# Gate and up products of the FFN by Strassen's scheme, with token pairs outside the weight chunks and the weights' low halves cut on GpSimd

## The reference

```python
def ffn(x, w_gate, w_up, w_down):          # x 2048 x 512, w_gate and w_up 512 x 2048, w_down 2048 x 512
    h = silu(x @ w_gate) * (x @ w_up)      # 2048 x 2048
    h = sparsify_2to4(h)                   # of each 4 neighbours in h the 2 largest magnitudes stay
    return layernorm(x + h @ w_down)
```

## Time and profile before

| | |
|---|---|
| time, median of 3 runs | 1092.13 us (1091.79 to 1092.42) |
| span of the profiled execution, first to last instruction | 1090.9 us |
| PE busy | 1037.0 us, 95% of the span |
| DVE busy | 738.5 us, 68% |
| ACT busy | 486.3 us, 45% |
| POOL busy | 294.7 us, 27% |
| mean granted TensorE clock | 0.992 of full speed |

### The profile page before, as it was taken

How to read it: one execution, slowest core, us unless ns; L and a number is a source line. 1 busy time by engine, 2 the same in 40 slices (tenths; PEclk the granted TensorE clock), 3 DMA queues, 4 the chain that set the end, 5 groups by cost and what they waited for, 6 DMA issues and landing times.

```text
span 1090.9 us, 18063 instructions
## 1 busy us (share of the span) xinstructions
PE 1037.0 (95%) x6022; PEld 839.6 (77%) x6023; DVE 738.5 (68%) x1769; ACT 486.3 (45%) x905; POOL 294.7 (27%) x496
## 2 busy tenths in 40 slices
PE   7889998999999885999999999999999999999996
PEld 6667776777777664888888888888888888888885
DVE  5898699778868986566747546545565536654666
ACT  5688488758857884222324222131222122221124
POOL 2186348545733641223210006000000000000224
PEclk9999999999999998999999999999999999999998
DMA  8877267727743732224541003210020000100102
GB/s 260 237 200 204 78 199 200 197 83 188 199 117 117 207 143 77 79 77 164 175 162 61 1 1 40 39 39 1 1 77 12 27 0 33 45 1 1 39 27 89
DMA packets 55216, 106.18 MB, mean 97 GB/s; under 512 B 6240, under 2 KB 8288, under 8 KB 55136
## 3 DMA queue, kind: packets, MB, share of 16 engines
q1 hardware_dynamic: 50256, 90.99, 29.7%
q0 software_dynamic: 4880, 14.18, 3.4%
HBM read 72.11 MB, written 30.94 MB: 94 GB/s over the span
## 4 chain that ended last, share of the span: by engine, by line
PE 57%; DVE 2%; ACT 1%; issue 0%; DMA 0%; POOL 0%; POOLq 0%; DVEq 0%
PE f_bank L53 55%; PE f_bank L1714 1%; PE f_bank L1722 1%; PE f_bank L1793 1%; PE f_bank L1738 0%; DVE ln_stats L1104 0%; DVE rows_kept L2150 0%; ACT rows_kept L1132 0%; DVE h L2116 0%; DMA rows<-sorted_dram 0%; DVE rows_kept L2139 0%; DVE h L2056 0%; DVE rows_kept L1111 0%; POOL out L1660 0%; ACT fsg L1936 0%
## 5 line engine op out<-in xcount | busy, mean ns | idle before, releaser
L1896 ACT ACTIVATE fsg<-f_bank 128x512 f32<-128x512 f32 x64 | 38.2, 598 | 295.6 <-PE f_bank L53 289.2
L2056 DVE TENSOR_TENSOR h<-f_bank,fsg 128x512 f32<-128x512 f32 x64 | 44.2, 691 | 181.6 <-PE f_bank L53 181.4
L714 ACT ACTIVATE probs<-bank,nmax 128x384 f32<-128x384 f32 (+3 forms) x256 | 131.7, 549 | 21.4 <-DVE nmax L899 19.3
L883 DVE CUSTOM_DVE_ANT_0 bank<-bank,mask 128x384 f32<-128x384 f32 (+3 forms) x256 | 122.9, 502 | 13.8 <-PE bank L510 13.0
L521 PE MATMUL bank<-ident,probs 128*128 128x128 f32 x640 | 108.7, 284 | 24.6 <-DVE pt_lo L908 10.7
L1137 POOL TENSOR_SCALAR ln_var<-ln_mv 128x1 f32<-128x1 f32 x39 | 8.9, 229 | 438.8 <-DVE ln_mv L1106 437.4
L908 DVE TENSOR_TENSOR pt_lo<-bank,pt_hi 128x512 f16<-128x512 f32 (+1 forms) x192 | 114.7, 598 | 16.7 <-ACT pt_hi L724 16.4
L724 ACT ACTIVATE pt_hi<-bank 128x512 f16<-128x512 f32 (+1 forms) x192 | 104.9, 546 | 23.5 <-PE bank L521 22.9
L53 PE MATMUL bank<-x_hi,w_qk 128*128 128x512 f32 x256 | 101.5, 414 | 6.7 <-DVE x_lo L913 6.3
L53 PE MATMUL f_bank<-wd_hi,hs_lo 128*128 128x512 f32 x256 | 100.0, 391 | 0.0
L53 PE MATMUL f_bank<-wd_lo,hs_hi 128*128 128x512 f32 x256 | 99.9, 390 | 0.0
(11 more groups left out here) (275 smaller groups left out, 2445.7 us busy)
## 6 DMA issues: line engine op xcount, KB each, us to landing
big_lo<-q_hi_dram SPq DMA_DIRECT2D x32, 256.0 KB
big_lo<-q_lo_dram SPq DMA_DIRECT2D x32, 256.0 KB
big_lo<-k_hi_dram SPq DMA_DIRECT2D x32, 256.0 KB, 3.8
big_lo<-k_lo_dram SPq DMA_DIRECT2D x32, 256.0 KB, 5.1
rows<-sorted_dram SPq DMA_DIRECT2D x19, 256.0 KB, 2.6
q_hi_dram<-q_hi SPq DMA_DIRECT2D x16, 256.0 KB, 3.0
q_lo_dram<-q_lo SPq DMA_DIRECT2D x16, 256.0 KB, 2.9
k_hi_dram<-k_hi SPq DMA_DIRECT2D x16, 256.0 KB, 3.5
```

What stands on the lines that cost most here:

```text
L714: ins = act.activation(probs[u % RP][:, at:at + cols(r)], S[u % SR][:, at:at + cols(r)], ACT.Exp, bias=nmax[:, r, c:c + 1])
L883: dve.tensor_tensor_reduce(out=S[u % SR][:, at:at + cols(r)], in0=S[u % SR][:, at:at + cols(r)], in1=mask[:, T - cols(r):T], scale=1.0, sc ...
L1896: act.activation(fsg[v % 2][:, :], GB[v % 2][:, :], ACT.Silu).then_inc(s_sg, 1)
L2056: dve.tensor_tensor(h[r % 2][:, j, :], UB[v % 2][:, :], fsg[v % 2][:, :], ALU.mult).then_inc(s_h, 1)
```

## The change

**Half-depth products.** For a pair of token blocks (r = 0, 1) and a pair of depth halves (each 256 of the 512 channels), the four products of gate and up against two token blocks are a 2x2 block product: weights (gate or up) by depth halves on one side, depth halves by token blocks on the other. Done plainly that is eight half-depth products; Strassen's scheme (in Winograd's form) makes it of seven, from sums and differences of weight blocks and of token blocks, and adds its results. A half-depth product here is 2 steps of depth by 3 matmuls, 6 matmuls. They are named 1 to 7, with a and b for two groups j; a round L holds 14 of them, 84 matmuls, where 96 stood for the same work. There are 16 rounds: 2 token pairs, by 4 chunks, by 2 halves of the groups.

**Order.** The token pair is now outermost, and each chunk's gate, up and down weights are loaded and cut twice, once for each pair. The tokens of the second pair are transposed, summed and cut between rounds 7 and 8. Down products come as 48 matmuls after the 14 products of a round: d = L - 2 after rounds 2 to 13, and the last four behind round 15. They use three PSUM banks in turn instead of four.

**ACT, for a round.** It copies six products out of PSUM (L2095), takes four SiLUs (L2100), makes magnitudes (L2112), copies the high half of what is kept (`kept_hi`, L2118, two of 1024 elements), and cuts 7 high halves of weights (`weight_hi`, L2046) for the next round and, in even rounds, 4 of down weights (`down_hi`, L2054).

**DVE, for a round.** Six additions of a product out of PSUM to a copy (`add_product`, L2288), two gated products with one input in PSUM (`gated_first`, L2295) and two with both in SBUF (`gated_second`, L2301), the comparisons, counts and choice of one block, the low half of what is kept (`kept_lo`, L2345, two of 1024), and four additions of the down product. It cuts no low halves of weights.

**GpSimd, for a round.** Four sums of weight blocks (L1729 to L1734) and seven low halves (`weight_lo`, L1739), and in even rounds four low halves of down weights (`down_lo`, L1747), each 128x512 with both inputs in SBUF. The raw weights have one buffer: the load of a round waits for the last low half of the round before.

**Buffers.** The high and low weights of a round have one place each, cut group by group (two products share a group) as PE is done with them.

The core of the diff, with the new functions:

```diff
-            def inner(c, v):
-                    matmul3(pe, banks[v % 2][:, :], lambda k, i: w[i][:, j, k, :], ..., KT).then_inc(s_done, 1)
+    ORDER = ("1a", "1b", "2a", "5a", "6a", "6b", "5b", "7a", "7b", "2b", "4a", "4b", "3a", "3b")
+    after_round = {L: [L - 2] for L in range(2, ROUNDS - 2)}
+    after_round[ROUNDS - 1] = [ROUNDS - 4, ROUNDS - 3, ROUNDS - 2, ROUNDS - 1]
+            def product(L, name):
+                for k in range(HALF):
+                    for a, b in ((0, 0), (0, 1), (1, 0)):
+                        ins = pe.matmul(to[:, :], aw[a][:, g, n, k * P:(k + 1) * P], x[b][:, k, :],
...
+            def down_product(d, ts=range(RW)):
+                    if t == 0:
+                        pe.wait_ge(s_hl, 2 * (d + 1))
+                        pe.wait_ge(s_dlo, J * (s + 1))
+            def weights_in(L):
+                if L > 0:
+                    sp.wait_ge(*wlo_ready(L - 1, GROUPS - 1))
...
+            def weight_sums(L):
+                pool.wait_ge(s_wraw, 64 * (L + 1))
+                pool.tensor_tensor(block_of(4), block_of(0), block_of(1), ALU.add).then_inc(s_wsum, 1)
+                pool.tensor_tensor(block_of(6), block_of(2), block_of(0), ALU.subtract).then_inc(s_wsum, 1)
...
+            def weight_lo(L, g):
+                i, j = group_blocks[g]
+                pool.wait_ge(s_whi, GROUPS * L + g + 1)
+                pool.tensor_tensor(aw[1][:, g, :, :],
...
+            def weight_hi(L, g):
+                act.wait_ge(s_wsum, 4 * (L + 1))
+                if L > 0:
+                    act.wait_ge(s_pr, NS + NPR * (L - 1) + 2 * g + 2)
...
+            def kept_lo(d):
+                for half in range(2):
+                    dve.wait_ge(s_hh, 2 * d + half + 1)
...
+            def round_(L):
+                add_product(L, "11a")
...
+                early(L)
+                add_product(L, "22a")
+                add_product(L, "22b")
+                add_product(L, "11b")
+                gated_first(L, 0)
+                gated_first(L, 1)
+                if L >= 2:
+                    kept_lo(L - 2)
+                add_product(L, "12a")
+                add_product(L, "12b")
+                gated_second(L, 0)
+                gated_second(L, 1)
+                if more:
+                    behind(L)
```

More of the change, by code:

```diff
@@ L1415, in cut_lo, with late @@
         dve.tensor_tensor(self.lo[:, e], self.raw[e], self.hi[:, e].bitcast(F32), ALU.subtract).then_inc(self.s_lo, 1)
[L1418 to L1455, removed]
+def late(nc, big_at, rows_kept, context, ident, tile_expert, slot_idx, place_idx, sorted_rows, s_sc, ordered_rows,
+         order_dram, gate, up, down, out_rows, N, E, D, I):
     KT = D // P
     NS = N // P + E - 1
-    RING = weights.RING
     RR = 4
@@ new lines, in late @@
+        y = [at(f"y{i}", [P, D], F32, arena + (28 + 2 * i) * KB) for i in range(2)]
+        sg = [at(f"sg{i}", [P, D], F32, arena + (32 + 4 * i) * KB) for i in range(2)]
+        gu = [at(f"gu{i}", [P, D], F32, arena + (34 + 4 * i) * KB) for i in range(2)]
+        ring = arena + 40 * KB
+        raw = at("w_raw", [P, 2, 2048], F32, ring)
+        aw = [at(f"w_{h}", [P, GROUPS, 2, HALF * P], F32R, ring + 16 * KB + 14 * KB * n) for n, h in enumerate(("hi", "lo"))]
+        kept = ring + 44 * KB
@@ L1620, in step @@
                     if n == EARLY:
[L1621 to L1622 removed]
                         block_in(0)
[L1624 removed]
+                    if n == EARLY + 2:
                         block_in(1)
[L1626 to L1635 removed]
             sp.wait_ge(s_sc, NT * 16)
@@ L1847, in _ @@
             tiles(pe, step)
-            chunks(pe, body)
-            for half in range(2):
-                outer(NCH - 1, NR - 1, half)
+            for L in range(ROUNDS):
+                for name in ORDER:
+                    if L == 0 and name in ("1a", "1b"):
+                        continue
+                    if L == 0 and name == "5a":
+                        last(expert_of(NS - 1), NS - 1, (NS - 1) % 2)
+                    product(L, name)
+                    if L == LB and name in ("2b", "4a", "4b", "3a"):
+                        boundary_turn(8 + ("2b", "4a", "4b", "3a").index(name))
+                if L == LB:
+                    boundary_turn(12)
+                    boundary_turn(13)
+                    down_product(L - 2, range(1))
+                    boundary_turn(14)
+                    boundary_turn(15)
+                    down_product(L - 2, range(1, RW))
+                else:
+                    for d in after_round.get(L, ()):
+                        down_product(d)
         @block.scalar
@@ L1867, in step @@
                 if where < 2 and later(n, 1):
                     x_hi(n + 1, 1 - i)
-                if isinstance(n, int) and n >= TURN:
-                    turned_hi(n - TURN)
+                if isinstance(n, int) and n in turns:
+                    for t in turns[n]:
+                        evict(t, XB[i])
+                if where == 2:
+                    act.wait_ge(s_ey, NS - 1)
+                    token_hi(0, "T1")
                 act.wait_ge(s_gT, n + 1)
@@ L1973, in _ @@
             tiles(act, step)
-            for p in range(RING, 2 * RING):
-                weights.cut_hi(act, p, p, weights.place(p, 0))
-            chunks(act, body)
+            token_hi(0, "T2")
+            token_hi(0, "T3")
+            for L in range(ROUNDS):
+                round_(L)
+            end = ROUNDS - 2
+            down_hi(STEPS - 1, range(J))
+            kept_hi(end)
+            magnitudes(STEPS - 1, 1, 0)
+            magnitudes(STEPS - 1, 1, 1)
+            kept_hi(end + 1)
             for half in range(2):
-                kept_hi(NCH - 1, NR - 1, half)
                 for n in (2 * half, 2 * half + 1):
@@ new lines, in pair, with compare @@
+            def pair(x, i, j):
+                return x[:, i:j + 1:j - i, :]
+            def compare(d):
+                m = mag[mag_of(d)]
+                dve.wait_ge(s_mag, 2 * (d + 1))
+                for i, first in ((0, 0), (1, 3), (2, 5)):
+                    w = J - 1 - i
+                    dve.tensor_tensor(beats[:, first:first + w, :], m[:, i:i + 1, :].broadcast_to([P, w, TW]),
+                                      m[:, i + 1:J, :], ALU.is_ge).then_inc(s_ch, 1)
+            b01, b02, b03, b12, b13, b23 = range(6)
```

919 lines of the change are left out of this document (554 added, 365 removed).

## The result

The change takes 1166.32 us (median of 4 runs, 1163.47 to 1167.65) where the kernel before took 1091.96 in runs on the same chip: a ratio of 1.068, with a 95% interval of 1.066 to 1.069. The direction was forecast, the size was not: 1140 was predicted, and 1166.3 lies 1.3 us above the range's upper end.

The account below looks back on a forecast made before the run. The prediction took PE's matmuls to bound the kernel. Stalls of 34.5 + 23 + 21 + 13 = 91.5 us against 43.5 of gain gave a span of 1138.9 and a forecast of 1140 us, range 1086 to 1165.

Parts of the forecast that it names:

- The gain: Gate and up products on PE: 192 fewer matmuls at 0.2267 us each, worth 43.5 us.
- Stall one: Down product waits because ACT's second SiLU stands behind high halves and cuts: 3.1 us in even rounds, 1.0 in odd.
- the port's share: Delay of DVE's kept low halves by taking turns with GpSimd on one SBUF port: 1.9 us a round.
- Stall two: DVE's kept low halves take turns with GpSimd's operations: 1.9 us more, making 5.0 in even rounds, 2.9 in odd.
- Opening, pair change and end: PE's stalls in the first rounds, around round 8 and at the last down products: 23, 21 and 13 us.
- The clock: PE's granted clock falling after waits near 9 us in rounds 2 and 8: up to 5 us each.
- Rival C: GpSimd keeps the port through its run of low halves: stalls 9.5 and 4.5 us, time 1166; chance 0.15.
- B: Port no obstacle, only the order of ACT's queue stalls PE: 42.4 us of stalls, time 1091; chance 0.18.
- D: Low halves ready before the 14 products end: no stalls, 7 us of start-up, time 1056; chance 0.09.

## Why the prediction was wrong

- **The gain, 43.5 us:** right as a count, 192 matmuls fewer (5830 against 6022).
- **Stall one, ACT's order:** right. With the port's share away, 3.01 and 0.93 us were measured for 3.1 and 1.0. In round 4 of the change the second SiLU ended 19.6 us after the round's first product began, for 19.0.
- **Stall two, DVE beside GpSimd:** right in mechanism and size. Even rounds waited 5.69 and three times 5.20 for 5.0, odd ones 3.55 and four times 2.73 for 2.9; the middle rounds sum to 21.3 + 14.5 = 35.8 us where 34.5 was forecast. The middle value of the 32 low halves was 2.28 us, which fits one operation of GpSimd in front of each.
- **Opening, pair change and end:** the mechanisms right, the sizes too high. Opening 2.57 + 6.37 + 6.99 + 0.85 + 3.25 + 1.33 = 21.4 us for 23, pair change 1.27 + 1.50 + 5.01 + 6.79 = 14.6 for 21, end 4.25 + 3.40 = 7.7 for 13, the last off by more than the third that was allowed. All added waits are 82.5 for 91.5.
- **The clock: the step that failed.** The prediction counted it for two waits near 9 us, up to 5 each outside the sum, and said "The shorter ones shouldn't." They did: sixteen waits, down to 2.73 us, cost 2.3 each on average, 36.0 in all, where the sum had nothing. 91.5 + 0 forecast, 82.5 + 36.0 measured; the difference of 27 us is that of the spans, 1165.9 and 1138.9; the 9 us too much in the waits hid a quarter of the miss. The kernel before could not show what short waits do: but for one at its very start, before PE's first matmul, it has no wait between 1.54 and 10.89 us. The price of one low stretch it did show, and the prediction misread it: the earlier trace rows were taken as some 12 us of low clock after the wait, but PE starts again at 425.03, and by the clock of 0.50 and 0.59 only some 4.3 us of its work were at half. That costs 2.1 us, not up to 5.
- **Rival C gave 1166** and the runs gave 1166.3, but by another cause: low halves did not wait for a run of GpSimd's, and waits of 5.2, not 9.5, stand in even rounds. The nearness is chance.
- **B and D:** out, by L2345 at 1990 ns and by the waits for it in each of rounds 2 to 6 and 8 to 13.

## What to carry to other kernels

When PE has no slack, price each new wait at its own length and then for the clock after it: here sixteen waits of 2.73 us and more cost 2.3 us each again, on average, and in these runs waits between 2 and 3.4 us went either way. A count of PE's matmuls says what a cheaper scheme can gain, but the chain from the last product that a step needs to the result that PE waits for decides; put what it waits for ahead of work that nobody needs yet, as the kept halves here (40 us). When one wait goes, look for what ends next before it: behind the kept low halves stood the low halves of the down weights. In these runs work on GpSimd was free for DVE where DVE's operation had an input in PSUM; with two inputs in SBUF on both, their times nearly added up.

## What was not expected of the hardware

PE's clock fell to half after waits of 3.85 us and more in a kernel made for it, after 2.73 in the change and after 1.97 in one of its variants, and of four equal waits of 3.01 us two were followed by half clock and two were not. A multiplication by a constant on DVE, with one input in SBUF, was slowed by GpSimd too: 12 of each took 16.7 us, 1.39 a pair, while DVE's last eight, alone, took (19.60 - 16.67)/8 = 0.37 each; GpSimd went from 1.22 to 1.39. The timeline rows of the two:

```profile
289.03 19.60 DVE L2310 TENSOR_SCALAR dve_out<-a 128x512 f32<-128x512 f32 x20 [2.86 <-POOLq L2327]
289.01 16.66 POOL L2324 TENSOR_TENSOR pool_out<-pool_a,pool_b 128x512 f32<-128x512 f32 x12 [0.18 <-DVEq L2308]
```
